# Source rows spread to all partitions by DMA through DRAM, in place of matmuls and casts, in the slot phase of a GNN kernel

## What is computed

```python
h = x @ enc_node_w + enc_node_b
e = edge_attr @ enc_edge_w + enc_edge_b
# each of the four layers:
msg = relu(h[src] + e) + 1e-7
m = msg * t
alpha = softmax of m over the edges that end at one node
agg = segment_sum(msg * alpha, dst)
out = h + agg
z = relu(layernorm(out @ w1 + b1)) @ w2 + b2
```

## Time and profile before

| | us |
|---|---|
| median of 3 runs | 6420.8 (6418.66 to 6430.37) |
| the profiled execution | 6423.57 |
| its span in the trace | 6419.1 |
| slot phase within the span | about 519 to 1791 |
| mean granted clock of TensorE over the span | 0.818 |

### The profile page before, as it was taken

The page is one execution under the profiler, slowest core; times in us unless marked ns, Lnnn a source line. Parts: engine busy times, 40 slices in busy tenths (PEclk is TensorE's granted clock), DMA queues, the critical chain, the costliest instruction groups (busy, mean ns, idle before and its releaser), DMA issues. The chain is left out here.

```text
span 6419.1 us, 112465 instructions
## 1 busy us (share of the span) xinstructions
PE 4606.3 (72%) x44676; PEld 3217.7 (50%) x44676; DVE 4837.2 (75%) x10914; ACT 1753.4 (27%) x2619; POOL 4403.1 (69%) x3850
## 2 busy tenths in 40 slices
PE   6716888899947777773777777377777746767776
PEld 6705778888834444442444444244444433444443
DVE  9432555544359999994999999499999958888887
ACT  2403778666611111110111111011111101111111
POOL 2054767666357777875777777477777747777776
PEclk8956988776668888886888888688888878888887
DMA  8962565544365555544555554445555534444442
GB/s 346 417 205 81 211 224 197 214 179 164 124 202 164 168 178 171 169 130 128 169 170 174 166 170 159 115 156 176 170 171 171 168 124 141 162 158 165 158 158 85
DMA packets 313907, 1116.65 MB, mean 174 GB/s; under 512 B 138994, under 2 KB 142244, under 8 KB 252308
## 3 DMA queue, kind: packets, MB, share of 16 engines
q1 hardware_dynamic: 163444, 839.13, 35.3%
q0 software_dynamic: 134800, 214.63, 13.7%
q10 hardware_dynamic: 15120, 55.50, 2.1%
HBM read 859.44 MB, written 249.52 MB: 173 GB/s over the span
## 5 line engine op out<-in xcount | busy, mean ns | idle before, releaser
L1228 POOL DMA_INDIRECT gb<-ztab,ovi x2704 | 3158.9, 1168 | 971.2 <-issue 825.2
L1326 PE MATMUL bank<-ep_mid,keep 128*128 128x512 f32 (+3 forms) x3474 | 1610.3, 623 | 18.0 <-DVE ep_mid L1316 18.0
L1326 PEld LDWEIGHTS bank<-ep_mid,keep 128*128 128x128 f32 x3474 | 709.6, 207 | 884.3 <-issue 819.5
L1379 PE MATMUL bank<-keep,na 128*128 128x128 f32 x100 | 47.5, 475 | 1028.6 <-DVE na L1376 1028.6
L1292 ACT ACTIVATE cm<-top_x,nt 128x64 f32<-128x64 f32 x196 | 68.2, 348 | 2569.7 <-DVE top_x L1286 2569.7
L1065 POOL DMA_INDIRECT ecell<-zpw,ptg x588 | 611.2, 1040 | 226.9 <-issue 177.1
L1243 PE MATMUL bank<-zpw,oh_mid 128*128 128x64 bf16 x21609 | 660.4, 194 | 108.8 <-DMA oh_mid<-ohd 102.9
L1243 PEld LDWEIGHTS bank<-zpw,oh_mid 128*128 128x128 bf16 x21609 | 656.2, 98 | 150.2 <-issue 139.6
L905 PE MATMUL bank<-byk,zpw 88*88 88x102 f32 (+13 forms) x4608 | 639.3, 314 | 17.1 <-DVE zpw L886 13.2
L905 PEld LDWEIGHTS bank<-byk,zpw 88*88 88x88 f32 (+13 forms) x4608 | 607.9, 216 | 22.9 <-DVE zpw L886 15.7
L1260 DVE TENSOR_TENSOR xb<-bank,xb 128x512 f32<-128x512 f32 x784 | 535.6, 686 | 90.5 <-DMA xb<-ecell 90.2
(11 more groups left out here) (222 smaller groups left out, 6604.6 us busy)
## 6 DMA issues: line engine op xcount, KB each, us to landing
oh_mid<-ohd SPq DMA_DIRECT2D x147, 1568.0 KB
oh_last<-ohd SPq DMA_DIRECT2D x49, 1568.0 KB
ea_in<-in_ea SPq DMA_DIRECT2D x101, 512.0 KB, 8.2
enc<-es_out ACTq DMA_DIRECT2D x101, 512.0 KB, 8.8
gb<-ztab,ovi POOLq DMA_INDIRECT x2704
ohd<-oh_lay SPq DMA_DIRECT2D x49, 576.0 KB
xb<-ecell SPq DMA_DIRECT2D x20, 1408.0 KB
ohd<-oh_lay SPq DMA_DIRECT2D x49, 512.0 KB
```

Source lines behind the costliest of these rows:

```text
L1228: at["g"][d] = ga_l[d % 2](GP.indirect_dma_start(gb[d % 2][:, 64 * v:64 * v + 64], None, T["ztab"], bass.IndirectOffsetOnAxis(ap=ovi[:, i: ...
L1326: q = PE.matmul(both[d % 2][:, 0:w], ident, rows[:, 128 * (c - a):128 * (c - a) + w], start=(c == 0), stop=(c + 4 >= S.S[d]), skip_group_c ...
```

## The change

The source numbers reach the partitions by DMA. For a block, `rows` makes them in fp32 (`lcf`), one TensorE transpose turns [128, 32] into [32, 128], ScalarE copies this to bf16 (`rowt`), SP stores it to a DRAM tensor (`rowc`, 8 KB), waits until it has landed, and loads it back to each of the 128 partitions (`cb`, now 8 KB in each partition, 1 MB in all, two buffers). `compares` waits on VectorE for that load, then compares eight groups at a time: 8, 7, 8, 8 and 1, the last three twice. The stores of the pieces are as before. In a unit the rows of both its blocks go first; then the scattered block's codes, the compares of the first block, the scattered block's rows, then the rest of the compares. L968 and L977 and their waits go. The steps for a unit fall from 35 to 20 (with a scattered block) and from 22 to 11 (without), and `share` follows.

```diff
-            lct = sb("lct", [128, G], BF16, yc)
-            idb = sb("idb", [128, 128], BF16, yc)
-            cb = sb("cb", [128, 4, 512], BF16, yc)
+            lcf = sb("lcf", [128, 2, G], FP32, yc)
+            rowt = sb("rowt", [128, 2, 128], BF16, yc)
+            cb = sb("cb", [128, 2, 128 * G], BF16, yc)
...
+            def rows(d, own):
+                n = n_rows[0]
+                n_rows[0] += 1
+                r = n % 2
+                if n >= 2:
+                    VE.wait_ge(pe_s, k["turn"][n - 2])
+                q = V(VE.tensor_tensor(lcf[:, r, :], own[:, 0:G], base, ALU.subtract))
+                k["split", d] = V(VE.tensor_copy(ovi[:, S.voff[d]:S.voff[d + 1]],
+                                                 own[:, G:S.S[d]]))
+                PE.wait_ge(ve_s, q)
+                if n >= 2:
+                    PE.wait_ge(ae_s, k["row"][n - 2])
+                k["turn"][n] = P(PE.transpose(bank[r][0:G, 0:128], lcf[:, r, :], ident))
+                AE.wait_ge(pe_s, k["turn"][n])
+                if n >= 2:
+                    awaits(AE, at["row"][n - 2])
+                k["row"][n] = A(AE.copy(rowt[0:G, r, :], bank[r][0:G, 0:128]))
+                SP.wait_ge(ae_s, k["row"][n])
+                if n >= 2:
+                    awaits(SP, at["cb"][n - 2])
+                    SP.wait_ge(ve_s, k["eq"][n - 2])
+                at["row"][n] = row_l[r](SP.dma_start(T["rowc"][r], rowt[0:G, r, :]))
+                awaits(SP, at["row"][n])
+                at["cb"][n] = cb_l[r](SP.dma_start(cb[:, r, :], T["rowc"][r:r + 1].rearrange(
+                    "o s i -> o (s i)").broadcast_to([128, 128 * G])))
+                return n, d
+
+            def compares(n, d):
+                awaits(VE, at["cb"][n])
+                for eight in eights:
...
+            def matrices(u, puts):
+                VE.wait_ge(ae_s, k["code"][u])
+                blocks = units[u]
+                ready = [rows(d, code[:, u % 2, M[u] * i:M[u] * i + S.S[d]])
+                         for i, d in enumerate(blocks)]
+                k["split"][u] = k["split", blocks[-1]]
+                yield
+                for j in puts:
+                    yield from pick(j)
+                    if len(ready) == 2:
+                        yield from compares(*ready.pop(0))
+                    ready.append(rows(S.put[j], pcode[:, 0:S.S[S.put[j]]]))
+                    yield
+                for r in ready:
+                    yield from compares(*r)
...
-                making = chained(*([put_matrices(n_put)] if put else []), unit_matrices(u))
+                making = matrices(u, [n_put] if put else [])
...
-                per = len(fours) + 2
-                share = 1.1 * (len(units[u]) * per + put * (per + 2)) / steps
+                share = 1.1 * (len(eights) * (len(units[u]) + put) + 4 * put + 1) / steps
```

More of the change, by code:

```diff
@@ L783, in lay @@
             k_z = V(VE.memset(z[:, 0, 64:128], 0.0))
-            k = {n: {} for n in ("kc", "kct", "ev", "hot", "spread", "put", "code", "bc", "cast",
+            k = {n: {} for n in ("kc", "kct", "ev", "hot", "spread", "put", "code", "turn", "row",
                                  "eq", "split", "ptg", "pick")}
[L786 to L789, removed]
+            at = {n: {} for n in ("cmb", "edge", "cell", "oh", "pcm", "prows", "sc", "row", "cb")}
+            n_fill, n_hot, n_rows = [0], [0], [0]
+            eights = [list(range(a, min(a + 8, S.singles))) for a in range(0, S.singles, 8)]
+            eights += [list(range(a, min(a + 8, G))) for a in range(S.singles, G, 8)]
             pieces = [0, S.singles, S.singles + 8]
@@ L956, in matrices @@
                 k["split", d] = V(VE.tensor_copy(ovi[:, S.voff[d]:S.voff[d + 1]],
                                                  own[:, G:S.S[d]]))
[L958 to L981, removed]
-                    yield
@@ L984, in compare @@
[L984 to L988, removed]
-                to = oh[:, 128 * S.ones[four[0]]:128 * S.ones[four[-1] + 1]]
-                if wide == 1:
-                    q = V(VE.tensor_scalar(to, wave, prow[:, 0:1], None, ALU.is_equal))
-                else:
-                    to = to.rearrange("p (a t i) -> p a t i", t=2, i=128)
-                    for t in (0, 1):
-                        q = V(VE.tensor_scalar(
-                            to[:, :, t, :], wave.rearrange("p (a i) -> p a i", i=128),
-                            prow[:, t:t + 1], None, ALU.is_equal))
-                k["eq"][m] = q
-                if four[-1] + 1 == (pieces + [G])[part + 1]:
-                    SP.wait_ge(ve_s, q)
-                    a, b = (128 * S.ones[(pieces + [G])[part + i]] for i in (0, 1))
-                    at["oh"][part] = oh_l[part](SP.dma_start(T["ohd"][d, :, a:b], oh[:, a:b]))
+                PE.wait_ge(ve_s, q)
@@ L1097, in put_matrices @@
                 k["pick"][j] = q
-                yield from matrices(d, pcode[:, 0:S.S[d]])
             def two_to_one(many, few):
@@ L1107, in two_to_one @@
                         yield
-            def chained(*parts):
-                for part in parts:
-                    yield from part
             scatters = scattering()
@@ L1160, in lay @@
                 pass
[L1161 to L1163 removed]
+            assert n_put == SCATTERED
             awaits(SP, *(at["cell"][u] for u in (last - 1, last)), *at["oh"].values(), at["z"],
```

36 lines of the change are left out of this document (22 added, 14 removed).

## The result

The changed kernel takes 6382.45 us, the median of 5 runs (6375.27 to 6386.91); the kernel before, timed beside it, takes 6419.77 us (6411.16 to 6430.37). The ratio is 0.994, with a 95% interval of 0.9925 to 0.9954: 37 us less by the medians, against 42 in the forecast. Timed again later in another group of runs it gave 0.9943 (0.9923 to 0.9962). The profiled execution took 6379.4 us with a span of 6375.1.

The account below looks back on a forecast made before the run. ScalarE was taken to bound the turns, TensorE the spreads of units 9 to 17, TensorE and VectorE those of 1 to 8. -80 + 15 + 12 + 3 + 4 = -46 us gave 6378 us; range 6312 to 6450.

Parts of the forecast that it names:

- The turns: Stretches where ScalarE is the bound: without casts 26.0 us each against 31.3; -80 us, ends -60 and -90.
- rival 3: Edge loads come late in the turns of seven units, 35 us go, no change: 6413 us; chance 0.14.
- Spreads of units 9 to 17: TensorE-bound stretches, all nine at 1.2 GHz: 401 us against 385.8, +15; units 9 to 12 lose, 13 to 17 gain.
- Spreads of units 1 to 8: Stretches limited by TensorE and VectorE: VectorE waits 1 to 4 us for `cb`, 33.5 us a unit, +12.
- rival 2: Units 1 to 8: slow `cb` load makes VectorE wait, emptying TensorE, spreads at 1.2 GHz: 6472 us; chance 0.17.
- The load: The 1 MB load of `cb` to all partitions: 5 to 8 us each; all 49 loads move 51 MB more.
- The row store: The 8 KB row on SP's queue behind the slot stores: 2.3 us after their 9.3.
- SyncE: SP stands still for each row's landing; users of the slot and piece stores queued behind have more time than that.
- The end: Unit 17's matrices have no cover: 27 to 29 us from the slot stores on; +4 us, ends 0 and +15.
- The rivals: 1: Spreads of units 9 to 12: the clock rises as before, so removed matmuls save 45 us: 6318 us; chance 0.13.
- 4: Spreads of units 9 to 17: steady business alone holds 2.4 GHz, 243 us in place of 401: 6220 us; chance 0.03.
- The sum: Whole kernel: -80 + 15 + 12 + 3 + 4 = -46 us, a time of 6378 us; chance 0.53.

Follow-up runs that it names:

- second execution: The changed kernel, unaltered, profiled again in a later group of runs beside the kernel before: 6379.9 us, ratio 0.9943.
- first execution: The changed kernel as profiled for the main result, against the kernel before: 6379.4 us, span 6375.1; median of the timed runs 6382.45 us, ratio 0.994.

## Why the prediction was right, point by point

**The turns**: forecast -80, measured -71 and -63. In units 9 to 16 it was close: 8 x 26.0 = 208 against 200.7 and 200.2, a drop of 43 where the forecast's half was 40. The experiment with the copies put back shows ScalarE's work as the cause, ScalarE full both times, and TensorE (22 us busy in 25) next, as said. In units 1 to 8 it fell short, 28 and 19 in place of 40. There ScalarE has its 205 us of work, as forecast, but stands idle for 23 and 32 us, since TensorE is late with the transposes. Two waits make it late, here over the whole slot phase of the second execution:

```profile
PEld bank L866 <- DMA edge<-enc,rpi: 16.7, 3, 9.0
PEld bank L854 <- DVE kc L844: 14.2, 5, 5.7
```

The first is rival 3 in small (13.6 us in the first execution, where turn 1 took 34.3 and turn 7 31.9 us, and 1.8 in before); the second is VectorE, late with the codes of the next unit. I had +3 for late edges and nothing for the codes.

**Spreads of units 9 to 17**: forecast +15, measured +24.6 and +22.1. I had all nine at 1.2 GHz throughout; eight were the first time and seven the second. That units 9 to 12 lose the fast clock for want of full-array matmuls came true, and so did the 44.6 us of an unbroken spread (44.4 in units 14 and 16). The miss is in units 13 to 17, which gave 8 us where 3 to 6 each were forecast. The term that was mis-sized is one I had put at nothing: holes. "VectorE has half its time free there" was true and did not help, since it waits in order. In units 13, 15 and 17 the left sides stand behind a compare that is late, and TensorE is idle 4.6, 3.4 and 2.9 us. The run without DRAM fills the holes of 13 and 17, and the store on ScalarE that of 15. (Unit 14 also gave less, since before it had 5 us at 2.4 GHz.) In unit 13 the load took 10.5 us, from 1392.38 to the compare at 1402.91, twice the usual, in the stretch in which GpSimd's edge fetches (issued at 1390.69 and 1391.94) went through the same 16 DMA engines, 0.94 and 0.99 busy (in the 10.5 us GpSimd's queue moved 2.95 MB beside the 1.06 MB of SP's):

```profile
1392.00:1397.00 5.00, 5.00 (x32) 5.00 (x31) 1.25 (x2) 1.28 (x3) 4.09 (x4) 0.50 0.94 331
1397.00:1403.00 6.00, 2.42 (x15) 2.15 (x13) 0.09 (x1) 0.85 (x2) 4.47 (x6) 0.50 0.99 407
```

That the fetches slow it is read from their place in time; no run took them away.

**Spreads of units 1 to 8**: forecast +12, measured +12.3 and +3.2. I had priced all eight alike, at 33.5, and the first execution's mean is 33.5: luck, since it is made of seven units at 32.8 and one at 39.0. In seven of them the sum is 229.3 and 221.8 us against 229.1, though unit by unit that is up to 4.1 more (units 2 to 4) and up to 5.9 less (units 1, 5 and 6). The increase is unit 8, 39.0 and 37.4 us against 26.9. The spread of unit 8, like those of 13 and 17, has two blocks' compares and no scattered block's codes: with no long code instructions ahead of the first compare, VectorE is there after a few steps and waits 8.8 and 9.4 us. The mechanism was rival 2's, in one unit of eight; in the others the waits for `cb` were 4.4 us (unit 2), 3.9 (unit 4), 0.7 (unit 7) or none, about the 1 to 4 forecast. The step that was missing is asking which units lack the cover.

**The load**: forecast 5 to 8 us. Measured from issue to VectorE: 4.7 at the end, 4.85 in unit 8, 5.2 in unit 7, 5.7 in unit 15, 10.5 in unit 13. The working from the store rows (4.7) was right where little or nothing shares the engines, and `smp` was the wrong neighbour. The slot phase moves the 51 MB more that were counted: the page's total goes from 1116.65 to 1168.18 MB.

**The row store**: taken as 2.3 us after the slot stores' 9.3. It was seen landed 9.0 us after its issue, with them rather than after them, and 5.0 us with nothing in front. At the end the first row was seen landed 10.3 us after the slot stores' issue (1724.60 to 1734.93), where 9.3 + 2.3 = 11.6 were forecast, and the load took 4.7.

**SyncE**: I wrote that the piece stores behind it have users with more time. VectorE waited 114 us for them in place of 4.7 (53 where no row goes through DRAM), and what it cost was small, as far as the windows show, because most of that lies in the turns.

**The end**: forecast 27 to 29 us from the slot stores on, measured 31.5. Against before it is +5.5 where +4 was forecast: from the stores on 8.1 more, ahead of them 2.7 less.

**The compare** of eight groups: forecast 0.50 us, measured 0.49.

**The rivals**: 1 did not come, though unit 10, and 11 the second time, rose for 10 us each. 2 and 3 came in one or two units each, for 12 and a few us. 4 did not come: unit 14 is 44.4 us of TensorE busy without a pause at 0.50.

**The sum**: -46 forecast. The rows that the change touches (turns, spreads, the end) add up to -29 and -32 us. The start of unit 1 gave -7 and +1 and the layers, which the change doesn't touch, -8 and 0; both are within what two executions of one kernel differ by (8.5 and 8.2 us between the two of the changed one). So the mechanism and the signs were right and the gain in the slot phase was a third smaller than forecast. That the median came within 5 us of 6378 is in part luck.

## What to carry to other kernels

Cut the trace by the units of the loop and price each kind of unit apart: the wait for the load was covered in most units that had long work queued ahead of it (unit 15 still lost 3 us) and cost up to 12 us in the kind that had none. A busy engine's clock is worth asking about before its instruction count: the whole change gave 0.6%, rows of zeros 2.1%. And a small transfer with a reader waiting is better issued from a queue that holds no large ones: here 5.2 us in place of 9.0 in unit 7, and a hole and 6 us at the end gone, though the 11 us in the whole time are at the edge of what the runs can tell.

## What the runs showed of the hardware that was not expected

The shape of TensorE's matmuls can decide its clock: with 88 x 88 fp32 matmuls, busy without a gap for 44 us, it stayed at 0.50 (units 14 and 16); with 40 rows of zeros added, the spreads of units 13 to 17 ran at a mean granted clock of 0.91 to 0.95 in the padded kernel before and 0.85 to 0.94 in the padded changed one. The Trainium skill, "TensorE: Matmul & The Clock Gate", Part 1, puts the clock down to how busy the engine has been recently. The traces here disagree, if "busy" is read as the time in which matmuls run.

A load in which all 128 partitions read one 8 KB row of DRAM took 4.7 us for 1 MB when alone and 4.9 to 5.2 beside small scatters. That is about the 4.7 us estimated for this size from the slot stores of before.

The standstills are no part of the kernel, since every kernel had them and one chip ran before once in 8138 and later in 6414 us. Unit 15's spread in the second run without DRAM shows one: between two groups of ten matmuls TensorE did nothing for 13.4 us, put down to VectorE, which was itself idle. Their cause was not found.
